# Experts' rows in half blocks of 64, two experts side by side in the column halves of the array

## The reference

```python
h = jax.nn.silu(xt @ w1 + b1) * (xt @ w2 + b2)      # per expert: 512 -> 128, twice
y = y + ge[:, None] * (h @ w3 + b3)                 # 128 -> 512, ge is 0 where not picked
```

## Time and profile before

| | us |
|---|---|
| median of 3 runs (lowest, highest) | 962.5 (962.22, 964.22) |
| the profiled execution: its own time | 964.04 |
| the profiled execution: its span | 962.3 |
| what lies around the span | 1.74 |
| PE busy in the span | 945.5 (98%) |
| DVE, ACT, POOL busy | 642.1, 411.1, 272.6 |
| stage of the blocks, first product to last output stored | about 855 to 956 |

### The profile page before, as it was taken

One profiled execution on the slowest core, in us unless ns is written; L12 is line 12 of the kernel. 1 busy time (PEld: TensorE's weight loads), 2 busy tenths in 40 slices (PEclk: granted clock), 3 DMA queues, 4 the chain that ended last, 5 costly groups with the idle time before them and its releaser, 6 DMA issues.

```text
span 962.3 us, 14020 instructions
## 1 busy us (share of the span) xinstructions
PE 945.5 (98%) x4863; PEld 788.8 (82%) x4863; DVE 642.1 (67%) x1073; ACT 411.1 (43%) x1004; POOL 272.6 (28%) x251
## 2 busy tenths in 40 slices
PE   9999999999999999999999999999999999999996
PEld 7888888888888788888888988989898877777773
DVE  6977679766665864653777778778787777843333
ACT  6336554333333342214556455464644425324442
POOL 1253424333433033003213131231311012043363
PEclk9999999999999999999999999999999999999998
DMA  7654554645556635548747646546465049565579
GB/s 261 227 208 175 191 192 154 230 171 211 179 204 208 220 146 193 213 143 310 267 171 283 224 142 223 210 154 229 140 220 199 27 178 340 195 205 180 170 199 262
DMA packets 86275, 193.75 MB, mean 201 GB/s; under 512 B 8608, under 2 KB 29344, under 8 KB 84800
## 3 DMA queue, kind: packets, MB, share of 16 engines
q1 hardware_dynamic: 76000, 171.64, 50.0%
q0 software_dynamic: 4272, 12.58, 5.1%
q10 hardware_dynamic: 5936, 8.65, 2.5%
HBM read 121.74 MB, written 71.11 MB: 200 GB/s over the span
## 4 chain that ended last, share of the span: by engine, by line
PE 90%; DVE 4%; issue 2%; POOL 1%; DMA 1%; ACT 0%; POOLq 0%; DVEq 0%; SPq 0%; ACTq 0%
PE ps_job L825 7%; PE ps_job L827 7%; PE ps_job L826 7%; PE ps_attn L1041 6%; PE ps_score L1013 6%; PE ps_attn L1282 4%; PE ps_score L885 3%; PE ps_turn L1027 3%; PE ps_score L886 3%; PE ps_score L887 3%; PE ps_attn L885 3%; PE ps_attn L887 3%; PE ps_attn L886 3%; PE ps_job L885 2%; PE ps_job L887 2%; PE ps_job L886 2%
## 5 line engine op out<-in xcount | busy, mean ns | idle before, releaser
L751 POOL TENSOR_TENSOR score_bias<-mask_bias,pos_bias 128x1024 f32<-128x1024 f32 x32 | 77.4, 2418 | 293.7 <-DVE probs L1849 185.3
L1336 ACT ACTIVATE probs<-probs,neg_max 128x128 f32<-128x128 f32 x256 | 99.5, 392 | 95.6 <-DVE neg_max L1852 95.6
L712 POOL TENSOR_TENSOR w_sum<-w_raw 128x256 f32<-128x256 f32 x30 | 22.8, 758 | 177.7 <-PE ps_attn L887 71.8
L1041 PE MATMUL ps_attn<-pT,v_s 128*128 128x128 f32 x512 | 62.7, 276 | 1.4 <-issue 1.1
L1282 PE MATMUL ps_attn<-ew_s,xbT 128*128 x248 | 62.6, 381 | 0.9 <-ACT xbT L1326 0.9
L1013 PE MATMUL ps_score<-kq_s 128*128 128x128 f32 x512 | 62.4, 275 | 0.0
L1041 PEld LDWEIGHTS ps_attn<-pT,v_s 128*128 128x128 f32 x512 | 59.8, 192 | 2.0 <-issue 1.2
L1282 PEld LDWEIGHTS ps_attn<-ew_s,xbT 128*128 128x128 f32 x248 | 44.6, 190 | 20.0 <-issue 15.0
L1013 PEld LDWEIGHTS ps_score<-kq_s 128*128 128x128 f32 x512 | 59.8, 192 | 0.2
L1876 DVE TENSOR_TENSOR acc<-ps_job,acc 128x512 f32<-128x512 f32 x56 | 37.9, 685 | 29.8 <-PE ps_job L827 29.7
L783 POOL DMA_INDIRECT xb<-x_rows,token_of x31 | 31.2, 1008 | 85.7 <-ACT y_out L1597 40.3
(11 more groups left out here) (469 smaller groups left out, 2593.5 us busy)
## 6 DMA issues: line engine op xcount, KB each, us to landing
kq<-st SPq DMA_DIRECT2D x32, 1024.0 KB, 4.2
kq_s<-kq SPq DMA_DIRECT2D x64, 512.0 KB, 4.5
v_s<-v_all SPq DMA_DIRECT2D x8, 2048.0 KB, 11.0
w_raw<-wa_dram SPq DMA_DIRECT2D x31, 512.0 KB, 5.6
v_all<-st SPq DMA_DIRECT2D x24, 512.0 KB, 3.7
y_slots<-ones SPq DMA_DIRECT2D x32, 256.0 KB, 4.7
wo_raw<-wo_dram SPq DMA_DIRECT2D x8, 1024.0 KB, 6.8
ew_s<-ew_dram SPq DMA_DIRECT2D x4, 2048.0 KB, 12.7
```

Of the source, the lines that this page charges most:

```text
L751: nc.gpsimd.tensor_tensor(score_bias[:], mask_bias[:], pos_bias[:, i % 2].unsqueeze(1).broadcast_to([P, B, P]), ALU.add).then_inc(bias_rea ...
L1041: last = nc.tensor.matmul(ps_attn[half][:, cols(b)], v_s[g % 2][:, BH * half + b, cols(j)], pT[:, half, cols(b)], start=True, stop=True)
L1336: last = nc.scalar.activation(probs[i % 2][:, half, b], probs[i % 2][:, half, b], ACT.Exp, bias=neg_max[:, i % 2, half, b:b + 1], accum_ou ...
```

## The change

The padding goes to half blocks of HB = 64 rows. 47 half blocks are enough for any routing, and two in a row make a pair: NB = 24 pairs, of which 35 half blocks, 18 pairs, hold rows with these picks. The rows of a pair are gathered, turned and copied together as before. The two halves may belong to two experts, so:

- `block_h` and `block_y` become two products for each one of before: rows 0 to 63 of the pair with one expert's weights into PSUM partitions 0 to 63, rows 64 to 127 with the other's into partitions 64 to 127. The columns streamed past each half are as many as before (256 and 512).
- PE and the first half address the first expert's weights where they lie. The second half reads a copy: DVE copies 128x1024 fp32 of `ew12_s` into `w12_b` and 128x512 of `w3_s` into `w3_b` for every pair, with the address from a register.
- DVE's bias add and ACT's output scaling become two instructions of 64 partitions; DVE and ACT load two owners for each pair, PE one.
- The order changes. In iteration b PE runs `turn_x(b + 1)`, `turn_h(b - 2)`, then `block_h(b)`, which now waits for the bias add of pair b - 1 (it stands behind the copy for pair b), then `block_y(b - 2)`. ACT takes y of pair b - 2, one iteration later than before.
- DVE copies the first pair's weights between the shared expert's adds 4 and 5, and the table that gives the owners is 1x768 in place of 1x512.
- `y_slots` is filled in 24 steps in place of 32; `y_pick` is one tile.

```diff
-NB = (TOP * T + E * (P - 1)) // P
+NHB = (TOP * T + E * (HB - 1)) // HB
+NB = (NHB + 1) // 2
...
-            def block_h(b, e, chunks):
+            def block_h(b, e):
                 k = b % 2
-                for c in chunks:
-                    last = nc.tensor.matmul(ps_attn[k][:, 0:2 * P], xbT[k][:, cols(c)], ew12_s[:, e, c],
-                                            start=(c == 0), stop=(c == C - 1))
+                for c in range(C):
+                    for half, w in enumerate((ew12_s[:, e, c], w12_b[k][:, c])):
+                        last = nc.tensor.matmul(ps_attn[k][half * HB:(half + 1) * HB, 0:2 * P], xbT[k][:, cols(2 * c + half, HB)],
+                                                w, start=(c == 0), stop=(c == C - 1))
...
-                nc.tensor.matmul(ps_job[k][:], hT_b[k][:], w3_s[:, e], start=True, stop=True).then_inc(yb_psum, 1)
+                for half, w in enumerate((w3_s[:, e], w3_b[k][:])):
+                    last = nc.tensor.matmul(ps_job[k][half * HB:(half + 1) * HB, :], hT_b[k][:, cols(half, HB)], w,
+                                            start=True, stop=True)
...
+            for b in range(NB + 2):
+                if b + 1 < NB:
+                    turn_x(b + 1)
                 if b >= 2:
-                    pe.wait_ge(hb_biased, b - 1)
+                    turn_h(b - 2)
+                if b < NB:
+                    owners.append(owner_of(b))
+                    pe.wait_ge(xbT_sbuf, b + 1)
+                    if b >= 1:
+                        pe.wait_ge(hb_biased, b)
+                    block_h(b, owners[b])
...
+                    block_y(b - 2, owners[b - 2])
...
+            def copy_w12(b):
+                V.tensor_copy(w12_b[b % 2][:], ew12_s[:, owners[2 * b + 1]])
+
+            def copy_w3(b):
+                V.tensor_copy(w3_b[b % 2][:], w3_s[:, owners[2 * b + 1]])
...
+                if b >= 2:
+                    take_hT(b - 2)
...
+                    copy_w3(b - 1)
                 if b + 1 < NB:
-                    owners.append(owner_of(b + 1))
-                dve.wait_ge(silu_b_done, b + 1)
...
+                    for half in range(2):
+                        owners.append(owner_of(2 * (b + 1) + half))
+                    copy_w12(b + 1)
+                if b < NB:
+                    dve.wait_ge(hb_psum, b + 1)
+                    for half in range(2):
+                        some = slice(half * HB, (half + 1) * HB)
+                        last = V.tensor_tensor(h_b[k][some, :], ps_attn[k][some, 0:2 * P], bias_all[some, owners[2 * b + half]],
+                                               ALU.add)
```

More of the change, by code:

```diff
@@ L372, in build @@
         gates_hi = place("gates_hi", [P, B, 1 + E], F32R, at_sums)
[L373 to L375 removed]
+        ended = place("ended", [1, 2 * NB, E], F32, at_rt)
+        w12_b = [place(f"w12_b{n}", [P, C, 2 * P], F32, at) for n, at in enumerate((at_rt, at_b3))]
+        assert C * 2 * P <= 11 * B * E
+        owner_f = small("owner_f", [1, 2 * NB])
+        owner = place("owner", [1, 2 * NB], I32, at_owner)
         round_up_i = small("round_up_i", [1, 2], I32)
```

129 lines of the change are left out of this document (61 added, 68 removed).

## The result

| | before | after |
|---|---|---|
| median us (lowest to highest, 4 runs each, one chip) | 962.58 (962.22 to 964.22) | 969.44 (967.96 to 970.8) |
| the profiled execution, its span | 964.04, 962.3 | 970.8, 969.1 |

The changed kernel is slower: ratio 1.0064, 95% interval 1.0050 to 1.0077, some 6 to 7 us. The forecast was 976.0 with a range of 965 to 995: right in sign and in range, twice too far in size.

What follows compares the result with a forecast made beforehand. PE bounds the blocks before (3.14 us a period); after, DVE's serial chain was to take 3.9 a pair. Picking up +14.2, end -2.5, port price +2 on the span of 962.3 gave 976.0; range 965 to 995.

Steps and rivals of the forecast that it cites:

- The chain and the sum's frame: The kernel's end hangs on 20 block periods, then POOL's picking up and last added transfer; terms +14.2, +2, -2.5 us.
- The start: Entry to the block loop: bias add 0 ends at 859.0 us, bias add 1 at 862.7.
- DVE's chain as the bound, 3.9: DVE's serial instructions in each pair, with two owner loads of 1.40 us uncovered, set a period of 3.9 us.
- rival 3: DVE's chain is half hidden, loads running ahead of their place: period 3.15 to 3.4, 961 to 967 us; chance 0.07.
- rival 4: DVE's loads and copies vanish under PE, which keeps 3.14 us a period: 959.9 us; chance 0.06.
- ACT's round, 3.3: ACT's silu, two loads, two outputs, store issue and `xbT` in each pair take 3.3 us, under DVE's 3.9.
- PE's 3.5: PE's period per pair with overlapping halves: 3.14 + 0.4 us for steps over, between 3.14 and 3.75.
- Rival 1: The halves don't run side by side on PE: period 5.72 us, 33 us more, 1009; chance 0.13.
- The picking up's start: POOL's first transfer of the picking up comes at 938.75 us against 924.56: +14.2.
- The port's price: POOL's transfers against DVE's SBUF copies, in first row loads and picking up: 2 us taken of a possible 7.
- The end: Seven fewer trailing iterations let DVE's final adds run before the last landing: -2.5 us.
- Path sees 20 periods: 31 blocks become 24 pairs, but the path keeps about 20 periods; the detour by block 30 goes, under 1 us.

## Why the prediction was right and wrong, point by point

**The chain and the sum's frame: right.** The end hung on the period, counted in 18 intervals, on the start, the picking up and the final adds, and the bookkeeping closes with these terms: +14.2 + 2 - 2.5 forecast, +9.7 + 1.1 - 4.0 measured.

**The start: right.** Forecast: bias add 0 ends at 859.0, bias add 1 at 862.7, first y store about 869. Measured: 859.4, 862.9, 869.19, the second of them by this row of DVE:

```profile
862.03 0.86 DVE L2153 TENSOR_TENSOR h_b<-ps_attn,bias_all 64x256 f32<-64x256 f32 x2
```

**DVE's chain as the bound, 3.9: the step that failed.** It took the two owner loads as 1.40 that nothing covers, placed behind the w3 copy's start. In the rows above DVE runs from one product to the next w12 copy in 897.25 - 895.75 = 1.50, with the product (0.29), the hT copy (0.29) and the w3 copy (0.42) in it: the loads begin beside them, and only 0.55 of them is uncovered (forecast: 0.99). With 1.50 + 0.61 to the bias adds + 0.85 + 0.4 for silu, DVE's own round is 3.36: the bound that the prediction named for one hidden load, 3.4, and rival 3, with a chance of 0.07. The step also closed the chain on DVE alone, with 0.38 for silu in every pair. Measured, the product waits 0.67 for silu on average (12.0 in 18 waits), since the chain runs on through ACT's loads, y and `xbT`: the loop of 7.27 for two pairs. The bound on rival 4 was misread as well: 3.15 to 3.26 less 2.9 leaves 0.25 to 0.36 for the two loads, not 0.6.

**ACT's round, 3.3: mis-sized, and the part that mattered.** From silu's start to y it had 0.2 + 0.85. The rows have 1.50 (895.40 to 896.90) and 1.24 in the next round; on average it is silu's 0.31 and an idle time of 0.93 (16.7 in 18). Rounds are 3.91 and 3.65 there, and 3.36 and 3.9 by turns elsewhere, 3.66 on average: 0.36 over the forecast, half of it between silu and y, the rest in y (1.38 for 1.3) and in small gaps. The moves of the loads show which engine's loads decide: ACT's alone 3.43, DVE's alone 3.55. The forecast had no case in which ACT bounds the pair. That 3.66 lies in its main case (3.5 to 4.3, "DVE-bound") and 969.4 in its range is luck.

**PE's 3.5: near 3.43 by luck, for another reason.** The skew of 0.4 for the order A, A, B, B does not exist: halves start 0.01 apart. The two drains, which the prediction kept out of its sum, cost 0.20, and 0.1 lies on the first product of h. Rival 1 (serial halves, 5.72) is ruled out; even the order written one half after the other gives 4.35.

**The picking up's start: +14.2 forecast, +9.7 measured.** 18 x (3.9 - 3.65) = 4.5 is the whole difference.

**The port's price: 2 forecast, 1.1 measured, and mostly of another instruction.** It was put on the weight copies. In the profile of after they cost 0.34 (the first three transfers, 1.23, 1.70, 1.08 in place of 1.04, 1.58, 1.05), and a final add, which the prediction counted as free once it leaves the queue, costs 0.77. The mechanism that the prediction took from the Trainium skill (SBUF — State Buffer, SBUF: two separate sides) holds as far as a transfer waits for an fp32 instruction of DVE that is under way. That page of the Trainium skill also has the one that starts first block the other fully; DVE's adds were not held by transfers under way, and there the rows decide; a w12 copy that began beside one took 0.88 in place of 0.69. The 7 us that the rule gave when applied to every copy were too many, since a copy costs only what is left of it when a transfer is issued.

**The end: -2.5 forecast, -4.0 measured.** The final add now ends 1.3 behind the last landing in place of 3.8: -2.5 as forecast. The output's last stores are two in place of a row of eight: 3.2 from the last add to the end in place of 4.6, which was not counted.

**"Path sees 20 periods": right for before, and the change gained by it.** The prediction put the detour by block 30 at under 1 us. The kernel before with 24 blocks shows it as 3.4, and with the shorter end a gain of 5.9 us, which the changed kernel has too. What it pays for the halves stands on top. In ratios: 0.9936 for 24 whole blocks in the old order; 0.9986 with copies, two owners and y one iteration later, still on the whole array; 1.0015 to 1.0020 with the halves; 1.0064 to 1.0090 with ACT's loads where the change put them. These ratios are of different chips, and the last two show how much that can make: a single step of 0.002 or 0.003 is better read from the periods.

## What to carry to other kernels

In a loop written out on several engines, add up every engine's instruction stream in order, loads into registers and issues of transfers too, and then look for loops that pass through two engines, which can be longer than an engine's own round: here DVE's alone was 3.36, the loop through DVE and ACT 3.64. Loads of 1.2 us in ACT's stream decided, and behind a long instruction of the same engine they cost nothing. Column halves of the array do run side by side, but a loop that changes between them and whole-array transposes pays for each change, and copies and second owners have to be paid by some engine. When work is taken off an engine's queue at the end, ask whom it will now run beside.

## What the runs showed of the hardware

- fp32 products of 128x64 in the two column halves start 0.01 us apart and keep the pitch of the whole array, 0.21 for 256 columns. With all of the first half's products ahead of the second's in the queue, the first half ran 0.92 us ahead, about four products.
- A change between whole array and column halves and back cost 0.20 us a pair.
- Two owner loads with their register work kept ACT idle for 0.65 to 1.18 us behind silu; a single load took 0.27 to 0.56 us. Moved behind y, beside 1.38 us of running instructions of the same engine, they cost nothing in the period.
- A GpSimd indirect transfer issued during DVE's fp32 add (1.22) or copy (0.69) in SBUF waits for it. Measured price: up to 1.04 for one transfer (2.59 in place of 1.55, in the kernel without copies). A transfer under way is not held and doesn't hold an add (1.22 to 1.25); w12 copies that began beside one took up to 0.98 in place of 0.69 (934.40 in the kernel with ACT's loads left out).
- On some chips DVE stood idle for 3 to 4 us between the first blocks in both kernels (3.75 and 2.98), which the trace puts down to nothing of the program. Where it comes from stays open. The kernel before took 966.5 in that batch in place of 962.6, and its profiled spans are 965.1 and 962.3.
- Behind 3.8 us without work for PE (860.25 to 864.03, the changed kernel's repeat) the granted clock was 0.50 (the 1.2 GHz level) from 866 to 868 and 1.00 again from 869 on; products of 256 columns then started 0.42 us apart.
